# Two attention layers: heads turned in two half-turns with the add done by transposes, and one over the softmax's sum on ScalarE

## The reference

```
x = layernorm(x + L0(x))   # TAG convolution, 5 hops, twice
x = layernorm(x + L1(x))   # mean over edges, then GATv2 attention with 4 heads and own row
x = layernorm(x + L2(x))   # graph convolution
x = layernorm(x + L3(x))   # GAT attention with 4 heads, then a dense layer
```

```
# L1, per edge e and head h; s2, d2 are source and destination, with a loop on every node
logit = einsum(leaky_relu(xl[s2] + xr[d2], 0.2), att)
a     = exp(logit - segment_max(logit)[d2]);  alpha = a / segment_sum(a)[d2]
out   = segment_sum(alpha * xl[s2]).mean(heads) + b_gat      # xl = h @ Wg_l + bg_l
out   = elu(layernorm(out) * gamma + beta)

# L3
coef  = ex / (segment_sum(ex)[dst] + 1e-16)
out   = (segment_sum(coef * (x @ W)[src]) + bias) @ dense_w + dense_b
```

## Time and profile before

| | us |
|---|---|
| median of the runs | 10212.91 |
| the profiled execution's own time | 10209.65 |
| its span | 10207.9 |
| softmax stage, layer 1 | about 7704.6 to 7766.5 |
| attention stage, layer 1 | about 7766.5 to 8434 |
| softmax stage, layer 2 | about 9523.7 to 9585.6 |
| attention stage, layer 2 | about 9585.6 to 10207.9 |

### The profile page before, as it was taken

How to read it: one execution, slowest core, us unless ns; L and a number is a source line. 1 busy time by engine, 2 the same in 40 slices (tenths; PEclk the granted TensorE clock), 3 DMA queues, 4 the chain that set the end, 5 groups by cost and what they waited for, 6 DMA issues and landing times. The chain is left out here.

```text
span 10207.9 us, 87159 instructions
## 1 busy us (share of the span) xinstructions
PE 5780.0 (57%) x19851; PEld 2971.5 (29%) x19851; DVE 5732.0 (56%) x16424; ACT 3186.3 (31%) x5395; POOL 6871.3 (67%) x6659
## 2 busy tenths in 40 slices
PE   1572455555555985555555500498886996710376
PEld 0231223333333542222222200143223553410143
DVE  2241455555555655666566668644448984520697
ACT  0352233333332332222222201244443662300144
POOL 7777777777777757777777777775760007767477
PEclk9796677777777996777777655699998997755698
DMA  4720232222225982223222222222333542222253
GB/s 127 203 91 20 75 110 88 91 86 90 88 90 140 261 230 83 87 86 90 86 88 87 82 75 80 69 72 57 74 70 98 165 143 68 76 49 53 81 152 123
DMA packets 1011155, 1016.67 MB, mean 100 GB/s; under 512 B 580468, under 2 KB 634086, under 8 KB 998090
## 3 DMA queue, kind: packets, MB, share of 16 engines
q1 hardware_dynamic: 797770, 880.58, 27.7%
q0 software_dynamic: 212864, 130.53, 7.3%
HBM read 491.67 MB, written 596.27 MB: 107 GB/s over the span
## 5 line engine op out<-in xcount | busy, mean ns | idle before, releaser
L717 POOL DMA_INDIRECT gathered<-u,place_of_source x1564 | 1639.7, 1048 | 520.1 <-issue 476.1
L717 POOL DMA_INDIRECT gathered<-hop,place_of_source x1564 | 1605.3, 1026 | 527.6 <-issue 490.5
L770 DVE SCALAR_TENSOR_TENSOR first_node_sum<-sums,ends_first,first_node_sum 128x64 f32<-128x64 f32 x4290 | 1203.5, 281 | 8.4 <-DVE sums L760 7.2
L746 DVE TENSOR_TENSOR weighted<-gathered,bank 128x512 f32<-128x512 f32 (+1 forms) x490 | 335.8, 685 | 1464.8 <-DMA gathered<-hop,place_of_source 644.1
L760 DVE SCALAR_TENSOR_TENSOR sums<-sums,same_as_before,weighted 128x64 f32<-128x64 f32 x3510 | 979.5, 279 | 61.8 <-DVE weighted L746 38.9
L717 POOL DMA_INDIRECT gathered<-x,row_of_source x782 | 804.9, 1029 | 298.5 <-issue 227.6
L2204 POOL DMA_INDIRECT out_dram<-lane_out,node_to_write x392 | 407.6, 1040 | 272.9 <-ACT lane_out L2125 156.8
L487 PE MATMUL bank<-dense_tmp,mean 128*128 128x512 f32 x980 | 519.7, 644 | 59.1 <-ACT dense_tmp L496 55.4
L487 PE MATMUL bank<-dense_a,center 128*128 128x512 f32 x588 | 440.6, 841 | 194.2 <-DVE dense_a L511 160.6
L717 POOL DMA_INDIRECT pair<-h_sage,row_of_source x391 | 403.4, 1032 | 217.9 <-issue 123.9
L717 POOL DMA_INDIRECT gathered<-y,place_of_source x391 | 403.9, 1033 | 192.2 <-issue 118.8
(11 more groups left out here) (461 smaller groups left out, 15433.2 us busy)
## 6 DMA issues: line engine op xcount, KB each, us to landing
head_sums<-head_sums SPq DMA_DIRECT2D x98, 1024.0 KB, 4.7
y<-conv_out SPq DMA_DIRECT2D x294, 256.0 KB
conv_out<-y SPq DMA_DIRECT2D x245, 256.0 KB, 3.0
hop<-sums SPq DMA_DIRECT2D x196, 256.0 KB, 2.1
turned<-rows_turned SPq DMA_DIRECT2D x196, 256.0 KB, 2.7
cat<-turned SPq DMA_DIRECT2D x196, 256.0 KB
u<-conv_out SPq DMA_DIRECT2D x196, 256.0 KB, 2.0
lane_raw<-x SPq DMA_DIRECT2D x196, 256.0 KB
```

The source lines that it names most:

```text
L717: return e.indirect_dma_start(out=into, out_offset=None, in_=tab, in_offset=bass.IndirectOffsetOnAxis(ap=index, axis=0), bounds_check=top, ...
L746: e.tensor_tensor(weighted[g % 2][:, 0:n, :], st.rows_of(g), over(st.weight[:, cols], D), ALU.mult).then_inc(st.weighed.handle, 1)
L770: e.scalar_tensor_tensor(h, row_, flast[:, t:t + 1], h, ALU.mult, ALU.add).then_inc(st.headed.handle, 1)
```

## The change

**Softmax.** The Exp is cut in two: over the edges' half as soon as VectorE has subtracted there, over the other half after the second subtraction. The reciprocal goes from VectorE to ScalarE as a Ln and an Exp with scale -1, and the products wait for it.

**Attention.** Steps 2 to 13 become 2 to 7, two times three. One half-turn brings both pairs of heads of half the columns into two banks: for each of 8 blocks a transpose of `heads` and a transpose of `head_sums` that accumulates on it. ScalarE copies both banks, then come two products (and the centred residual in the second). So VectorE's additions (L2263, L2266) and the semaphore `ended` are gone; the first half-turn waits for `owned` and `summed` itself. The second bank of a half-turn is bank 4 or 7 in layer 1 (alternating) and bank 4 in layer 2. In layer 1 the shares are read from `logits` directly, without the copy into bank 7. Layer 2 has 4 slots of `head_sums`. The chains are 25 and 16 steps, and the shift between lanes is a third of that.

```
-        HD = 14
+        HD = 8
         LAST = HD + (GAT_STEPS if v2 else 6)
-        NS = 4 if v2 else LANES
+        NS = 4
...
+        more = (PS[4], PS[7]) if v2 else (PS[4],)
...
+                if v2:
+                    return lg[:, :, g * K8:(g + 1) * K8]
...
-                return at(g, 12)
+                return at(g, 6)
+
+            def heads_tensor(e, W, g):
+                j = g // LANES
+                o, s = (a[:].rearrange("p k d -> p (k d)") for a in (O[g % 5], S[g % NS]))
+                for q in range(2):
+                    if q:
+                        yield W.n(j, 5)
+                    e.wait_ge(*W.at(j, 0, 2 + 3 * q))
+                    for c, b in enumerate((W.bank[0][0], more[g % len(more)])):
+                        for n in range(4):
+                            at_ = slice(n * 2 * W4 + q * W4 + c * P, n * 2 * W4 + q * W4 + (c + 1) * P)
+                            to = b[:, n * P:(n + 1) * P]
+                            e.matmul(to, o[:, at_], ident[:], start=True, stop=False, is_transpose=True)
+                            m = e.matmul(to, s[:, at_], ident[:], start=False, stop=True, is_transpose=True)
+                    m.then_inc(W.chain[0].handle, 1)
+                    yield W.n(j, 4 + 3 * q)
+                    e.wait_ge(*W.at(j, 0, 4 + 3 * q))
+                    for c in range(2):
+                        m = e.matmul(W.bank[0][1][:, :], stack_w[:, c, q, :], W.b(f"gt{c}", 0), start=q + c == 0, stop=q + c == 2 and v2)
+                    if q and not v2:
+                        m = e.matmul(W.bank[0][1][:, :], wts["center"][:], W.b("xT", 0), start=False, stop=True)
+                    m.then_inc(W.chain[0].handle, 1)
+
+            def heads_scalar(e, W, g):
+                j = g // LANES
+                for q in range(2):
+                    yield W.n(j, 3 + 3 * q)
+                    e.wait_ge(*W.at(j, 0, 3 + 3 * q))
+                    for c, b in enumerate((W.bank[0][0], more[g % len(more)])):
+                        m = e.copy(W.b(f"gt{c}", 0), b[:, :])
+                    m.then_inc(W.chain[0].handle, 1)
...
-                    e.wait_ge(*ended(g + 1))
...
+                    e.wait_ge(*owned(g + 1))
+                    e.wait_ge(*(fixed(1) if g == NG - 1 else summed((g + 1) * K8 - 1)))
+                    if g >= len(more):
+                        e.wait_ge(*at(g - len(more), 7))
+                    yield from heads_tensor(e, W, g)
...
-                        if v2:
-                            m = e.tensor_tensor(o[:, :, P:W4], o[:, :, P:W4], s[:, :, P:W4], ALU.add)
-                        else:
-                            for k in range(0, K8, 2):
-                                m = e.tensor_tensor(o[:, k:k + 2, :], o[:, k:k + 2, :], s[:, k:k + 2, :], ALU.add)
-                        m.then_inc(ended.handle, 1)
```

More of the change, by code:

```diff
@@ L1915, in softmax_terms @@
         V = {n: i + 1 for i, n in enumerate(
-            "fences scans ends own front back merged level shifted run met others all before behind inverse shares".split())}
+            "fences scans ends own front back merged level edges_shifted shifted run met others all before behind shares".split())}
         levelled = sem("levelled", 1)
-        sv, stn, sa = sem("softmax_vector", len(V)), sem("softmax_tensor", 3), sem("softmax_scalar", 1)
+        sv, stn, sa = sem("softmax_vector", len(V)), sem("softmax_tensor", 3), sem("softmax_scalar", 4)
         with ExitStack() as ctx:
@@ L1945, in _ @@
                 def _(e):
+                    e.wait_ge(*sv(V["edges_shifted"]))
+                    e.activation(lg[:, 0:HEADS, n], lg[:, 0:HEADS, n], ACT.Exp).then_inc(sa.handle, 1)
                     e.wait_ge(*sv(V["shifted"]))
-                    e.activation(lg[:], lg[:], ACT.Exp).then_inc(sa.handle, 1)
+                    e.activation(lg[:, HEADS:, :], lg[:, HEADS:, :], ACT.Exp).then_inc(sa.handle, 1)
+                    e.wait_ge(*sv(V["behind"]))
+                    e.activation(mf[:, :, n], mf[:, :, n], ACT.Ln).then_inc(sa.handle, 1)
+                    e.wait_ge(*sa(3))
+                    e.activation(mf[:, :, n], mf[:, :, n], ACT.Exp, scale=-1.0).then_inc(sa.handle, 1)
                 @block.vector
@@ L2001, in _ @@
                     e.wait_ge(*sv(V["met"]))
+                    e.wait_ge(*sa(2))
                     e.scalar_tensor_tensor(mb[:, :, n], lg[:, HEADS:, n], tiny, lg[:, 0:HEADS, n], ALU.add,
@@ L2013, in _ @@
                     m.then_inc(sv.handle, 1)
-                    e.wait_ge(*sv(V["behind"]))
-                    e.reciprocal(mf[:, :, n], mf[:, :, n]).then_inc(sv.handle, 1)
-                    e.wait_ge(*sv(V["inverse"]))
+                    e.wait_ge(*sa(4))
                     e.tensor_tensor(lg[:, 0:HEADS, n], lg[:, 0:HEADS, n], mf[:, :, n], ALU.mult)
@@ L2077, in rows_tensor @@
                     yield W.n(j, 2)
-                    e.wait_ge(*ended(g + 1))
-                    for i in range(4):
-                        q, c = i // 2, i % 2
-                        def part(l_, n):
-                            lo = n * 2 * W4 + q * W4 + c * P
-                            return O[g % 5][:].rearrange("p k d -> p (k d)")[:, lo:lo + P]
-                        if v2 and c == 0:
-                            yield W.n(j, 2 + 3 * i)
-                            e.wait_ge(*W.at(j, 0, 2 + 3 * i))
-                            for n in range(4):
-                                lo = n * 2 * W4 + q * W4
-                                to = W.bank[0][0][:, n * P:(n + 1) * P]
-                                e.matmul(to, part(0, n), ident[:], start=True, stop=False)
-                                m = e.matmul(to, S[g % NS][:].rearrange("p k d -> p (k d)")[:, lo:lo + P], ident[:], start=False, stop=True)
-                            m.then_inc(W.chain[0].handle, 1)
-                        else:
-                            yield from turn_tensor(e, W, j, 2 + 3 * i, part)
-                        yield W.n(j, 4 + 3 * i)
-                        e.wait_ge(*W.at(j, 0, 4 + 3 * i))
-                        m = e.matmul(W.bank[0][1][:, :], stack_w[:, c, q, :], W.b(f"gt{c}", 0), start=i == 0, stop=i == 3 and v2)
-                        if i == 3 and not v2:
-                            m = e.matmul(W.bank[0][1][:, :], wts["center"][:], W.b("xT", 0), start=False, stop=True)
-                        m.then_inc(W.chain[0].handle, 1)
+                    e.wait_ge(*owned(g + 1))
[3 more added lines that the diff above has]
+                    yield from heads_tensor(e, W, g)
                     if v2:
@@ L2111, in rows_scalar @@
                     yield from turn_scalar(e, W, j, 0, "xT")
-                    for i in range(4):
-                        yield from turn_scalar(e, W, j, 2 + 3 * i, f"gt{i % 2}")
+                    yield from heads_scalar(e, W, LANES * j + l)
                     if v2:
@@ L2220, in move_shares @@
                         e.tensor_copy(shares(g), lg[:, :, g * K8:(g + 1) * K8]).then_inc(shared_.handle, 1)
-                    move_shares(0)
+                    if not v2:
+                        move_shares(0)
                     for g in range(NG):
@@ L2277, in _ @@
                     steps = steps_of(rows_tensor, e)
-                    steps.to(due(NG - 1, 0.8))
+                    last = (NG - 1) // LANES * STEPS + (NG - 1) % LANES * APART
+                    steps.to(due(NG - 1, 0.8) if v2 else last + 2)
                     e.wait_ge(*summed(T - 1))
+                    e.wait_ge(*at(NG - 1 - len(more), 7))
                     e.matmul(PS[4][:, 0:W4], link[:], S[(NG - 1) % NS][:, K8 - 2, :], start=True, stop=True).then_inc(carried.handle, 1)
```

18 lines of the change are left out of this document (8 added, 10 removed).

## The result

The changed kernel took 10163.63 us, the median of 5 runs (10160.84 to 10170.9), against 10212.91 for the kernel before in 5 runs (10200.96 to 10214.27). The ratio is 0.9955 with a 95% interval of 0.9942 to 0.9967: 46 us faster, 34 to 59 by the interval, and 49 by the medians. Forecast were 10139 and 74 us, in a range of 10080 to 10195. The sign, the place and the mechanism came out; a third of the gain did not.

A forecast was written before the change was run, and what follows sets the result against it. Layer 1 was taken as bound by the round trip TensorE, ScalarE, TensorE, layer 2 and both softmax stages by VectorE; 19.3 + 34 + 20.4 = 73.7 us off 10209.65 gives 10136, at the runs' median 10139; range 10080 to 10195.

The forecast's parts named there:

- Softmax, 19.3 us: Both softmax stages: reciprocal replaced by ScalarE's Ln and Exp, scans starting earlier; 9.6 us saved a layer, 19.3 in both.
- about 55 us from the fences to the first loads: Softmax stage: sign that the forecast is right, its length after the change, with no reciprocal on VectorE.
- Layer 1, 34 us: First attention layer: group 12.35 us against 12.92, saving 26.8 us over 47 groups, with first turn and tail 34.
- Issue: 40 x 0.11 + 7 x 0.86 = 10.35 us: Layer 1 group: TensorE's time for 40 transposes and 7 large matmuls, before 1.95 us of stalls.
- First turn: Start of the first attention layer: the first turn comes 1.2 us earlier.
- tail: Layer 1, from the turn of group 47 to the last output: 41.4 us instead of 47.6, 6.2 saved.
- Layer 2, 20.4 us: Second attention layer: group 11.3 us against 11.65, TensorE late instead of VectorE; 20.4 us saved.
- (a): Rival, both attention layers: stalls better hidden, floors of VectorE 11.2 and GpSimd 10.6 us decide; 10058; chance 0.14.
- (b): Rival, both attention layers: TensorE loses its clock; 10212 at a mean grant of 0.93, 10305 at 0.85; chance 0.09.
- (c): Rival, attention: unchanged, since one more unseen round trip eats the rest; softmax gain only, 10193; chance 0.12.
- (d): Rival, head turns: an accumulating transpose costs like an identity matmul, 3.8 us more a group; 10510; chance 0.03.
- The clock: TensorE in both attention layers: full rate, 2.4 GHz, taken despite the skill's rule that transposes do not count as activity.

The follow-up runs named there:

- Experiment 11: Experiment 7's kernel with one of each group's eight scatters in the second attention layer; that stage 492.2 us to the last copy.
- experiment 3: Changed kernel, the second half's turns not waiting for TensorE's own products of the first half; ratio 0.9979 to the kernel before.
- experiment 4: Changed kernel, each half's first product waiting for the first copy alone; ratio 0.9955 to the kernel before.
- experiment 9: Changed kernel with one of each group's eight GpSimd scatters in the second attention layer; that stage 585.3 us to the last copy.
- experiment 7: Changed kernel with experiments 3 and 4 together and turns announced to ScalarE bank by bank; ratio 0.9952 to the kernel before.
- experiment 8: Changed kernel with its 32 adding transposes a group as plain products by the identity; 12378.3 us in one run.
- experiment 1: Kernel before with the changed softmax alone; 12077.3 against 12090.6 us, ratio 0.9988.
- experiment 2: Kernel before with the changed softmax, and the changed attention in the first layer only; ratio 0.9955.
- experiment 10: Kernel before with the changed softmax and one of each group's eight scatters in the second attention layer; that stage 593.6 us to the last copy.
- experiment 12: Kernel before with the changed softmax and experiment 7's first attention layer; 10107.7 against 10213.4 us, ratio 0.9894.
- experiment 5: Changed kernel again without edit, beside the kernel before on another chip; ratio 0.9995.

## Why the forecast was right, and where it was 25 us off

**Softmax, 19.3 us: right.** 9.7 and 9.8 us; a piece of Exp or Ln took 1.507 us, where I took 1.5. One of the signs did not follow from this sum: "about 55 us from the fences to the first loads" should have been 61.96 - 9.6 = 52.4, and 52.3 was measured.

**Layer 1, 34 us: the mechanism right, one term too small.** The group was to take 12.35 us and takes 12.63. Row by row: the stall behind the first turns is 0.47 (0.45 forecast), the wait for its own products 0.32 (0.32), the stall behind the second turns 0.89 (0.87), the last mean 0.30 (0.3). What is not in the sum is what comes after a stall. From the waiting products to the next matmul of another kind it is 1.82 us (8007.06 to 8008.88), not 1.72; from the waiting mean to the next turn 0.97, not 0.86. Their records show it: 1.98 and 1.12 us, where products and means that did not wait have 1.88 and 1.02. It is the first pass over the 512 columns that is longer: between 7900 and 8300 us all 63 passes of L2102 that stand behind a stall took 0.70 us and the next pass began 0.53 us after their start; passes that had not waited took 0.59, and the next began after 0.43. The kernel before had such rows too (1.13 at 8004.39 in the earlier trace rows), and I took my price from the ones beside them that had not waited. These two make 0.21 us. Another 0.04 are in the two stalls, 0.04 at the turns that wait, and 0.07 are plain arithmetic: 40 x 0.11 + 7 x 0.86 is 10.42, not 10.35. That is 0.36 over the sum of 12.30, where 0.33 was measured. The term of the forecast that was too small is "Issue: 40 x 0.11 + 7 x 0.86 = 10.35 us": each matmul behind a stall takes 0.10 us more than it allows, and the rest is its arithmetic. Little cancelled this: the softmax, the first turn and the tail came out a little better than forecast (0.2, 0.2 and 1.5 us), the groups of both layers short of it. Experiment 11, whose products never wait in layer 2, runs at exactly such a sum (9.52 against 9.56).

From the turn of group 0 to that of group 47 the changed kernel takes 8377.79 - 7780.49 = 597.3 us, 9.8 less than before, where 26.8 was forecast. Of the 17 us that are missing, 47 x 0.28 = 13 are this term, and some 2 are at the start, where the first four groups take 44.3 us in both kernels (by VectorE's products); the other 2 I have not placed. First turn (1.4 us earlier, 1.2 forecast) and tail (39.3 us for 47.0 between the same starts, so 7.7 less where 6.2 was forecast) came out.

The forecast thought that a product with its shares in SBUF might take 0.5 us more, hidden in VectorE's wait. It takes 2.28 us (L2277 over 7900 to 8300), as from a bank, so that cost is not there.

**Layer 2, 20.4 us: the same term.** 11.51 us in place of 11.3: two products a group wait and cost 0.10 more each (9851.25 to 9853.07 is 1.82), and 40 x 0.11 + 6 x 0.86 is 9.56, not 9.5. Measured by the scatters, the period fell from 11.65 to (10118.21 - 9599.89)/45 = 11.52, so 45 x 0.13 = 6 us come from the groups; the other 6 come from the first scatter, which is that much earlier.

**The bound: right, and shown.** I had said that TensorE's trips to ScalarE, not VectorE's load, set the pace of layer 1. Taking 0.28 us a group of such waits away gave 16.3 us (experiment 3), taking 0.98 away 43.5 (experiment 4), with no compute instruction less on any engine. VectorE's 1.3 us a group of waiting was slack. In layer 2 the same is shown by experiments 9 and 11: with as few scatters in both, the waits taken away bring a group from 11.51 to 9.52 us.

**Rivals.** (a) failed as a forecast of this kernel, but its floor of 11.2 us for VectorE is what experiment 7 reaches in layer 1 (11.15 to 11.26). (b) did not come: the clock is 1.00 in both windows. Its words and its sum do not agree: "all but the softmax's gain is gone" would be 10193, and its 10212 is the sum with the softmax's gain used up as well. (c) was nearest to what is missing: a cost at the round trips that I had not seen, but one that eats a third of the gain and not all of it. (d) is refuted by the single records, and experiment 8 shows its price.

**The clock.** In layer 1 4.4 of 12.6 us a group and in layer 2 4.4 of 11.5 are transposes, more than before, and the granted clock was 1.00 in both windows, 2.4 GHz. In layer 2 it had been 0.94, with idle stretches of 3.08 us ahead of a turn that are gone now. The rule of the Trainium skill that spoke against the forecast ("TensorE: Matmul & The Clock Gate", Part 4: PE-mode transposes do not count as activity for the full clock) would, as the forecast read it, have lengthened the groups. With transposes and matmuls mixed like this no trace shows that; no run has a stage of transposes alone, so the rule itself is not refuted.

**What stays open.** On chips B and C the second stage is longer in the changed order (657.9 and 647.0 us, both on C) than in the old one (620.1 and 631.4, both on B). On one and the same chip there are only experiments 3 and 4 against 1 and 2: the changed order with waits taken away took 657.1 and 662.9 us on B. The next section has what was seen. That GpSimd's scatters bring it was to be tested by experiments 9 and 10, and they ran on a chip without it. That the old order suffers less because VectorE, and not TensorE's round trip, bounds it is argued, not shown.

## What to carry to other kernels

When a change trades VectorE work for matmuls in a pipeline of fixed order, walk TensorE's order and add the trips to the engine that empties its banks; here those waits, and 0.1 us for each matmul behind one, decided the group, not the busy shares. Then look at what each wait really needs: a half's first product needs only the first copy, the first copy only the first bank, and no turn needs its own engine's last product; in the first layer that was worth 68 us on top of the change's 19. And measure on more than one chip before a stage that lives on tight round trips is called faster.

## What the runs showed of the hardware

**Chips differ, by stage.** Two chips took 12087 to 12091 us for the kernel that takes 10213 in the result and in experiments 9 to 12, while the first attention stage is as long on all of them. In experiment 5's second attention stage ScalarE starts a copy long after TensorE has turned its bank. The last of 16 transposes starts at 11516.90 and lasts 0.27 us; ScalarE's row is

```profile
11518.72 1.07 ACT L2113 COPY lane_gt<-bank 128x512 f32<-128x512 f32 x2 [2.56 <-remote]
```

which is 1.55 us after the end. I took this distance, as far as ScalarE was idle in it, for every copy to lane_gt in 400 us that ScalarE had waited for. On the first chip (9700 to 10100) it is 0.04 us for all 70 in the changed kernel and for all 68 in the kernel before. In experiment 5's window of 11450 to 11850 19 of 61 are over 0.5 us, the longest 2.9; in experiment 1's 28 of 84 are, the longest 2.8. In the first layer of experiment 5 (9600 to 10000) all 63 are 0.04. What makes the starts late is not shown.

**A late start is paid twice on TensorE.** Behind that copy TensorE had been idle for 2.23 us, and its products ran at half rate. These are its row and the windows of the idle stretch and of what follows, with a granted clock of 0.54, near the lower level of 1.2 GHz:

```profile
11519.84 3.58 PE L2102 MATMUL bank<-lane_gt,g_stack 128*128 128x512 f32 x4 [2.23 <-issue]
```

```profile
11517.50:11519.80 2.30, 0.11 (x2) 0.00 (x0) 2.12 (x6) 1.08 (x3) 1.33 (x2) 1.00 0.05 16
11519.80:11523.30 3.50, 3.46 (x5) 1.38 (x6) 3.06 (x3) 0.99 (x2) 1.41 (x2) 0.54 0.61 225
```

The first of the two windows shows more than TensorE idle: the DMA share is 0.05, where VectorE is busy for 2.12 of 2.30 us. Stalls of up to 0.73 us, as in the changed kernel's steady groups, left the clock at 1.00.

**A transpose of one fp32 matrix can add to a bank,** at 0.11 us for each 128x128 piece, half of what a matmul by the identity costs (0.22).
